# Fourier mixing stage of a two-block network: weights loaded in eight pieces per unit, X and MLP weights loaded earlier, last scatters issued by three engines

## The reference

```python
xn = _layernorm(x, norm1_w, norm1_b)
xf = jnp.fft.rfft2(xn, axes=(1, 2), norm='ortho').reshape(B, h, w // 2 + 1, NB, BS)   # 8 blocks of 24
o1 = jnp.einsum('bhwni,hwnio->bhwno', xf, w1c) + b1c          # w1: (32, 17, 8, 24, 24, 2)
o1 = jax.lax.complex(relu(o1.real), relu(o1.imag)).reshape(B, h, w // 2 + 1, C)
xs = jnp.fft.irfft2(o1, s=(h, w), axes=(1, 2), norm='ortho')
hdn = gelu(_layernorm(xs, norm2_w, norm2_b) @ mlp_w1 + mlp_b1)          # 192 -> 768
return xs + x + hdn @ mlp_w2 + mlp_b2
```

## Time and profile before

| | |
|---|---|
| runs of the kernel | 1224.67 us median of 3 (1222.74 to 1226.86) |
| profiled execution | 1229.31 us, its span 1227.1 us |
| PE busy | 1092.4 us (89%), 9256 matmuls |
| DVE, ACT, POOL busy | 854.0 (70%), 697.0 (57%), 365.5 (30%) |
| mean granted TensorE clock | 0.943 |
| weight queue q1 | 131160 packets, 37.12 MB |
| queue of kind "instruction" q8 | 55 packets, 0.90 MB |
| DMA over the whole span | 64.18 MB, mean 52 GB/s |

### The profile page before, as it was taken

One profiled execution on the slowest core, in us unless ns is written; L12 is line 12 of the kernel. 1 busy time (PEld: TensorE's weight loads), 2 busy tenths in 40 slices (PEclk: granted clock), 3 DMA queues, 4 the chain that ended last, 5 costly groups with the idle time before them and its releaser, 6 DMA issues. The chain is left out here.

```text
span 1227.1 us, 26088 instructions
## 1 busy us (share of the span) xinstructions
PE 1092.4 (89%) x9256; PEld 885.9 (72%) x9256; DVE 854.0 (70%) x2230; ACT 697.0 (57%) x1293; POOL 365.5 (30%) x388
## 2 busy tenths in 40 slices
PE   2549898998578799999979999999999699999998
PEld 1238887887247688899847777767766488989887
DVE  4735544453389988777759769869789767676665
ACT  2545554563365466766676666577554366666665
POOL 1150011111289900000125716527436411111110
PEclk9868888898789899999989999999999889999999
DMA  8977799976300000000010000000000000000001
GB/s 162 317 178 113 142 159 159 151 148 197 82 21 1 1 0 0 0 0 0 0 46 1 1 1 1 1 1 1 1 1 1 0 13 26 26 26 26 26 26 38
DMA packets 138553, 64.18 MB, mean 52 GB/s; under 512 B 114176, under 2 KB 133280, under 8 KB 138464
## 3 DMA queue, kind: packets, MB, share of 16 engines
q1 hardware_dynamic: 131160, 37.12, 16.4%
q0 software_dynamic: 5728, 19.22, 5.9%
q10 hardware_dynamic: 1584, 6.72, 1.7%
HBM read 44.17 MB, written 12.58 MB: 46 GB/s over the span
## 5 line engine op out<-in xcount | busy, mean ns | idle before, releaser
L880 ACT ACTIVATE L_conv_hf<-L_conv_ps,L_conv_b 128x512 f32<-128x512 f32 x192 | 132.0, 688 | 183.4 <-PE L_conv_ps L1051 175.5
L1070 PE MATMUL L_conv_ps<-w2hl,L_conv_hhi 128*128 128x384 f32 x768 | 228.1, 365 | 3.6 <-DVE X L966 3.6
L956 DVE TENSOR_TENSOR L_conv_hlo<-L_conv_hf,L_conv_hhi 128x512 fp32r<-128x512 f32 x192 | 141.3, 751 | 78.1 <-ACT L_conv_hhi L889 75.4
L1070 PE MATMUL L_conv_ps<-w2hl,L_conv_hlo 128*128 128x192 f32 x768 | 188.5, 252 | 0.0
L1185 POOL TENSOR_TENSOR sc_lo<-XS,sc_hi 128x512 fp32r<-128x512 f32 x96 | 142.8, 1503 | 116.4 <-ACT sc_hi L1261 116.4
L1463 PE MATMUL sc_ps<-sc_hi,wh 128*128 128x512 f32 (+1 forms) x440 | 161.0, 437 | 3.4 <-ACT XS L1245 3.2
L621 PE MATMUL psF<-spectrum,X 100*24 100x64 f32 x4352 | 129.5, 290 | 23.7 <-issue 20.2
L1070 PEld LDWEIGHTS L_conv_ps<-w2hl,L_conv_hhi 128*128 128x128 f32 x768 | 144.4, 188 | 7.3 <-DVE L_conv_hlo L956 2.7
L1463 PE MATMUL sc_ps<-sc_hi,wl 128*128 128x512 f32 (+1 forms) x440 | 147.9, 393 | 0.0
L621 PEld LDWEIGHTS psF<-spectrum,X 100*24 100x24 f32 x4352 | 121.6, 122 | 34.9 <-issue 34.7
L1070 PEld LDWEIGHTS L_conv_ps<-w2hl,L_conv_hlo 128*128 128x128 f32 x768 | 146.2, 191 | 0.0
(11 more groups left out here) (135 smaller groups left out, 2052.0 us busy)
## 6 DMA issues: line engine op xcount, KB each, us to landing
X<-in_L_conv_w SPq DMA_DIRECT2D x34, 576.0 KB
XS<-in_x POOLq DMA_DIRECT2D x8, 768.0 KB, 8.2
rows_spectrum<-XS POOLq DMA_DIRECT2D x8, 768.0 KB, 6.7
d<-rows_spectrum ACTq DMA_DIRECT2D x8, 768.0 KB, 7.4
XS<-d POOLq DMA_DIRECT2D x64, 96.0 KB, 6.3
X<-in_x SPq DMA_DIRECT2D x8, 768.0 KB, 6.8
out<-X SPq DMA_DIRECT2D x15, 384.0 KB, 2.6
spectrum<-in_L_conv_mlp_w SPq DMA_DIRECT2D x2, 576.0 KB, 6.0
```

The costliest lines, as they stand in the source:

```text
L880: nc.scalar.activation(hf[:, m % 3, :], ps[:, RB + m % 2, :], gelu, bias=b1[:, m:m + 1]).then_inc(act1, 1)
L956: nc.vector.tensor_tensor(hlo[:, m, :], hf[:, m % 3, :], hhi[:, m, :].bitcast(F32), ALU.subtract).then_inc(h_lo, 1)
L1070: mm = pe.matmul(o, x, w, start=(m == 0 and n == 0), stop=(m == MT - 1 and n == 1), skip_group_check=True)
```

## The change

The weights of a unit go out in eight pieces (four row ranges for each of the two halves), the bias with the first two. `mixed` now counts eight steps per unit, one per 32 products, and piece i of unit u waits for step i of unit u - 2. The pieces of unit 0 wait for the row copies of slabs 4 to 7, those of unit 1 for the second spectrum load. In the last units four slabs of X are issued during the products of unit 15 and the MLP weights during those of unit 16. The other four slabs of X are loaded in inverse_rows, where SP gets a part. The scatters of the last group are issued by SP (three), POOL (three) and ACT (two), each with a semaphore `last_in[k]`; all scatters of the other groups of one parity share one semaphore. Every wait on `mixed` is rescaled. Three lines whose condition is never met are dropped.

```diff
-            sp.wait_ge(x_in[XT - 1], 16)
-            for u in range(UNITS):
+            def load_piece(u, i):
+                r, k, rows = u % RING, i % 2, slice(H // 4 * (i // 2), H // 4 * (i // 2 + 1))
+                s, at = (k, WF - 1) if units[u] is None else (units[u][1], 2 * units[u][0] + k)
+                into = Wt[r][:, k].rearrange("p h o r -> p h (o r)")
+                sp.dma_start(into[0:HALF, rows], w_v[s, at][:, rows]).then_inc(w_in[r], 16)
+                if i < 2:
+                    sp.dma_start(into[HALF:HALF + NH], b_v[s, at]).then_inc(w_in[r], 16)
+
+            for i in range(STEP):
+                sp.wait_ge(d1_done, 2 * TPB + 2 * i)
+                load_piece(0, i)
+            sp.wait_ge(d2_in[1], 16)
+            for i in range(STEP):
+                load_piece(1, i)
+            for u in range(2, UNITS):
+                for i in range(STEP):
+                    sp.wait_ge(mixed, STEP * (u - 2) + i + 1)
+                    load_piece(u, i)
...
-            for u in range(UNITS - RING, UNITS):
-                sp.wait_ge(mixed, 2 * (u + 1))
-                if u == UNITS - 2:
-                    for dst, src in sh.mlp_loads("L0_conv_"):
-                        sp.dma_start(dst, src).then_inc(sh.raw_in, 16)
-                again(u)
+            for n, (u, half) in enumerate(itertools.product((UNITS - 4, UNITS - 3), range(2))):
+                sp.wait_ge(mixed, STEP * (UNITS - 2) + 2 * n + 1)
+                again(u, half)
+            for n, (dst, src) in enumerate(sh.mlp_loads("L0_conv_")):
+                sp.wait_ge(mixed, STEP * (UNITS - 1) + n + 1)
+                sp.dma_start(dst, src).then_inc(sh.raw_in, 16)
+            sp.wait_ge(d3_v, 2 * NG)
+            sp.wait_ge(d3_a, 2 * NG)
+            for k in (0, 3, 6):
+                scatter(sp, NG - 1, k)
...
-                for k in range(TPB):
-                    pool.dma_start(XS[g:P:NG, B * k:B * (k + 1), :].rearrange("p b c -> p (b c)"),
-                                   d3[g % 2][k:P:TPB, :]).then_inc(sh.rows_in[g % 2][k], 16)
+                for k in range(TPB) if g < NG - 1 else (1, 4, 7):
+                    scatter(pool, g, k)
...
+            for k in (2, 5):                      # ACT, after waits for d3_v and d3_a
+                scatter(act, NG - 1, k)
...
-                    if hl % 8 == 7:
+                    if hl % 2 == 1:
                         mm.then_inc(mixed, 1)
...
+        @block.sync                               # in inverse_rows
+        def _(sp):
+            for k in range(TPB):
+                sp.wait_ge(sh.last_in[k], 16)
+            for r in (0, RING - 1):
+                for k in (2 * r, 2 * r + 1):
+                    sp.dma_start(sh.X[:, B * k:B * (k + 1), :], x_v[k]).then_inc(sh.x_back[r], 16)
```

More of the change, by code:

```diff
@@ L149, in __init__ @@
         self.raw_in = self.sem("raw_in")
-        self.rows_in = [[self.sem(f"rows_in{k}_{t_}") for t_ in range(TPB)] for k in range(2)]
+        self.rows_in = [self.sem(f"rows_in{k}") for k in range(2)]
+        self.last_in = [self.sem(f"last_in{t_}") for t_ in range(TPB)]
     def load_table(self, n, func):
@@ L314, in col_bank, with scatter @@
             return 6 if u == 1 else 4
+        def scatter(eng, g, k):
+            eng.dma_start(XS[g:P:NG, B * k:B * (k + 1), :].rearrange("p b c -> p (b c)"),
+                          d3[g % 2][k:P:TPB, :]).then_inc(sh.last_in[k] if g == NG - 1 else sh.rows_in[g % 2], 16)
         block = ctx.enter_context(nc.Block())
@@ L327, in _ @@
                 sp.dma_start(spectrum[k][HALF:HALF + NH, :], t["block_ones"][HALF:HALF + NH, :]).then_inc(ones_in, 16)
-            sp.wait_ge(x_in[XT - 1], 16)
-            for u in range(UNITS):
-                r = u % RING
[L332 to L338, removed]
@@ L437, in rectify @@
                 for q in range(2):
-                    act.wait_ge(mixed, 2 * u + q + 1)
+                    act.wait_ge(mixed, STEP * u + STEP // 2 * (q + 1))
                     nc.scalar.activation(
@@ L446, in inverse_out @@
                 if g >= 2 and half == 0:
-                    for k in range(TPB):
-                        act.wait_ge(sh.rows_in[g % 2][k], 16 * (g // 2))
+                    act.wait_ge(sh.rows_in[g % 2], 16 * TPB * (g // 2))
                 nc.scalar.activation(d3[g % 2][:, 384 * j:384 * j + 384], ps[:, 7, 0:384], ACT.Copy).then_inc(d3_a, 1)
@@ L551, in inverse_out @@
                 if g >= 2 and half == 0:
-                    for k in range(TPB):
-                        dve.wait_ge(sh.rows_in[g % 2][k], 16 * (g // 2))
+                    dve.wait_ge(sh.rows_in[g % 2], 16 * TPB * (g // 2))
                 nc.vector.tensor_copy(d3[g % 2][:, 384 * j:384 * j + 384], ps[:, 6, 0:384]).then_inc(d3_v, 1)
@@ L609, in products @@
                 r = u % RING
-                pe.wait_ge(w_in[r], 64 * (u // RING + 1))
+                pe.wait_ge(w_in[r], 16 * (STEP + 2) * (u // RING + 1))
                 spread_done(u)
@@ L683, in inverse_rows @@
         loads, splits = sh.mlp_loads("L0_conv_"), sh.mlp_splits()
+        x_v = t["x"].rearrange("b (t hh) w c -> t (hh w) b c", hh=HH)
         block = ctx.enter_context(nc.Block())
+        @block.sync
[5 more added lines that the diff above has]
+                    sp.dma_start(sh.X[:, B * k:B * (k + 1), :], x_v[k]).then_inc(sh.x_back[r], 16)
         @block.tensor
         def _(pe):
+            for s in range(2):
+                pe.wait_ge(sh.rows_in[s], 16 * TPB * (NG // 2 - s))
             for k in range(TPB):
-                for s in range(2):
-                    pe.wait_ge(sh.rows_in[s][k], 16 * NG // 2)
+                pe.wait_ge(sh.last_in[k], 16)
                 passed(pe, xs_done, 4 * (k - 1))
```

17 lines of the change are left out of this document (7 added, 10 removed).

## The result

| | before | after |
|---|---|---|
| median of the runs | 1223.70 us | 1198.68 us (1196.19 to 1201.1, 4 runs) |
| ratio | | 0.9774 (95%: 0.9749 to 0.9798) |
| profiled span | 1227.1 us | 1194.4 us |
| start to first product matmul | 89.97 us | 78.75 us |
| first to last product | 213.0 us | 192.9 us |

The change gains 2.3%, or 25 us by the medians (before is four runs here, the three shown ahead and one more). The two profiled executions differ by 32.7 us in their spans: before's profile took 1229.31, longer than any of its four timed runs, and after's is the fastest of its four. So some 8 us of that difference are the choice of executions. In stages the 32.7 are 11.2 + 20.1 + 2.7 - 1.4, up to rounding.

The account below looks back on a forecast made before the run. PE was taken as the bound, slowed by waiting for its own instructions behind weight packets. Savings of 4 + 2.5 + 14.5 - 1 + 4 = 24 us from the median 1224.67 gave 1201 us, range 1190 to 1210 (chance 0.48).

Parts of the forecast that it names:

- the signs promised: Slabs under 6 us apart, first columns near 74, issue near 12, clock above 0.9, last copy to inverse rows near 10.
- Row stage and hand-over: Before the first products: holding weights back saves 4 us on the x slabs and 2.5 us on spectrum landings.
- Units: Products, columns, inverse halves: pieces shrink the weight pile delaying PE's instructions, saving 14.5 us (bounds 34 and -5).
- The two halves of the term: In the units: 7.5 us fewer holes at the products and 7 us less clock loss.
- Odd units: In odd units, which also carry spectrum load and scatter, holes halve from 15.4 us; even units keep 4.8.
- Last units: Units 15 and 16: more X and MLP bytes beside the products cost 1 us; other X loads stay hidden.
- End: Last copy to inverse rows: POOL issues three scatters instead of eight and reaches its DRAIN earlier, gaining 4 us.
- three readings of the DRAIN: At the end: DRAIN lasts 10.08 us from its start, gain 2.4; ends 3.5 after last landing, 6; neither, 9.
- A: In the units: holes vanish altogether, saving 34 us instead of 14.5, for 1181 us; chance 0.17.
- B: In the units: holes stay, as busy DMA engines as such delay the fetch; only 9.5 us gained, 1215; chance 0.22.
- C: In the units: pieces load too slowly and PE waits for weights, 67 us in all, for 1282 us; chance 0.08.
- D: Whole kernel: nothing measurable, gains vanish or holes move to other units, 1222 to 1228 us; chance 0.05.

Follow-up runs that it names:

- e1: The kernel before, with only the weights of units 0 to 3 held back, still as whole transfers; ratio 0.9956, 1221.39 us.
- e2: The changed kernel with units 0 to 3 loaded at the old early start, without pacing; 1200.80 us, ratio 0.9801.
- e3: The changed kernel with all eight pieces of a unit issued at its first step, without pace; 1195.98 us, ratio 0.9768.
- e5: The kernel before with each 576 KB weight transfer cut into four of 144 KB at the old time; 1207.82 us, ratio 0.9858.
- e10: The changed kernel with the four early slabs of X issued as sixteen quarters of 192 KB at the same steps; 1198.38 us, ratio 0.9759.
- e4: The changed kernel with the weights of units 4 to 16 left out; 1190.08 us (one run).
- e7: The changed kernel with all eight slabs of X loaded in the inverse rows; 1192.08 us, ratio 0.9719.
- e8: The changed kernel with the scatters of the last two groups issued by SP and ACT, none by POOL; 1190.68 us, ratio 0.9708.

## Why the prediction was right or wrong

The time was 1198.7 where 1201 stood, and the signs promised came: slabs under 6 us apart (5.97), first columns near 74 (69.7 here, 74.7 on average over the seven kernels with the same late start), "issue" near 12 (11.2), clock above 0.9 (0.93), no wait for a DMA at the products, and a weight queue that runs through them (below, 104 to 108 us). Two were missed: there is still idle time before slabs 5 and 6, and from ACT's last copy to the first inverse-row matmul it is 11.5 us where near 10 stood (14.2 before).

```profile
q1 hardware_dynamic: 3392, 0.64, 91.8%
q8 instruction: 1, 0.02, 1.5%
```

The sum was right partly for wrong reasons, and partly by luck. Its terms were worked out against the profile of before, and in the profiled pair they come to 32.7 instead of 24; the medians of the runs give 25.

**Row stage and hand-over, -6.5.** Right in size, and 11.2 in the profile, where after has the earliest first product of all kernels. Over the profiles of all kernels the first product stands at 89.3 us on average with the early start (89.97, 88.36, 87.56, 87.32, 93.17; 576 KB pieces only in the first) and at 84.0 with the late one (78.75, 82.59, 84.54, 86.36, 86.70, 83.69, 85.50): 5.3, with 6 to 8 between the kernels of each kind. e1, with a late start of whole transfers, has 87.58 and gives 5 alone. The slabs account for less of it than the 4 us that stood: from slab 3 to slab 7 they are on average 6.1 us apart with the late start of the pieces and 6.5 with the early one. What the step left out is the price: units 2 and 3 now load beside units 0 and 1, so that e2, with the early start, is hardly slower than after (2 us by the medians, within the noise).

**Units, -14.5.** It was -20 in the profiled pair (the last units among them), and the mechanism failed in one step. That PE waits for blocks of its instructions beside DMA traffic is right. The step that failed is that such a block waits behind the pile of weights, and that pacing shrinks the pile to one piece. e3 drops the pace and loses nothing; e5 has the old time and the old pile and has the gain. What counts beside the weights is the size of the transfer: the holes go 20.2, 13.2, 8.0 from 576 to 144 KB.

How the size does it stays open. Transfers of 576, 288 and 144 KB take some 3.4, 1.7 and 0.9 us, an estimate from 3072 packets per 576 KB at about 900 per us, and the order of the delays fits a block that waits for the transfer it met. But with pieces of 144 KB the packet's start is still up to 2.3 us late, units 3 and 9 left out, the DMA share falls with the size as well, and e10 speaks against making it a rule for all transfers. The Trainium skill (DMA: Bandwidth & Descriptors, Queues, rings and completion order) lets an engine take turns between queues at packets of some 9 to 17 descriptors; by that the size of a transfer should not matter, and from 576 to 144 KB it mattered by 12 us of holes.

The two halves of the term were both too small. The holes gave 9.0 instead of 7.5, and the clock 11.1 of busy time instead of 7; by the column groups alone, whose excess over 1.99 us fell from 12.4 to 4.6, it is 8.

**Odd units.** Here the step was wrong, and an error the other way hid it in the total. The holes of the odd units were to halve, from 15.4, and those of the even ones to stay at 4.8. In after the odd units have 3.1 left (1.08, 0.28 and 1.78), and the even ones 8.1, of which 4.89 are unit 16's and 1.66 unit 12's. So the drop of "issue" from 20.2 to 11.2, near the 12 forecast, is a sum of -12.3 and +3.3. What remains in units 3 and 9 stands beside the spectrum load: the start of the instruction packet is late there by 1.9 to 4.2 us in all thirteen profiles, and by 2.2 and 1.9 even in e4, where it costs 0.9 us of holes in all. The prediction took unit 1's hole of 1.11 for one beside weights alone; a spectrum load was issued at 103.5 and was moving then too.

**Last units, +1.** Wrong by size: the hole in unit 16 went from 2.15 to 4.89, and e7 puts the price of the X slabs there at 6.6 us by the medians. The other half of that step, the loads hidden in the inverse rows, was right and could have been used for all eight slabs.

**End, -4.** It gave 2.7. Of the three readings of the DRAIN the second is nearest: it ends some 4 to 5 us after the last landing of POOL's own transfers. Before, that is 318.8 and 323.4; after, 284.8 and 289.2; in e8, 269.9 and 273.8. Over all thirteen profiles it is 3.9 to 5.5 us, while the DRAIN is 9.1 to 15.4 long. The step took 314 for the last landing, 4.4 us behind ACT's last copy; it was 284.8, 6.6 behind, as the premise that group 6's scatters are gone by then was false: they stood in POOL's queue ahead of group 7's. The rule of the Trainium skill cited there (DMA: Bandwidth & Descriptors, Issuing engines are not separate DMA queues), that issuing from several engines saves only sequencer time, misses this: taking POOL out of the last two groups is worth 6.7 us, as its DRAIN then ends beside other work.

**The rivals.** A (holes vanish) did not come; e7 comes near it, with 3.4 us of holes and 1192.1. B (the holes stay, whatever the form of the traffic) did not come, and e5 speaks against it; that the share of busy engines plays a part is not excluded, since the share fell with the size. C (pieces too slow) did not come: no product waits for weights, at 72 KB neither, though SP then issues for some 10 us of each unit. D did not come.

## What to carry to other kernels

Where an engine with many small instructions shows gaps that end by "issue", ask what the DMA engines carry at that moment: try smaller transfers first (144 KB instead of 576 KB took 1.4% off this kernel without moving any), then move bulk loads to a stage with idle DMA, as the inverse rows here. Read the packets of kind "instruction" beside the gaps: they tell whether a block came late and what moved before it. Ahead of a barrier, keep the last transfers off POOL: here its DRAIN ended only 4 to 5 us after the last of them had landed. When a pace and a size are changed in one edit, cross them before you credit either: here the pace got the credit in the forecast and the size did the work.

## What the runs showed of the hardware that was not expected

- An instruction block of PE is delayed by other traffic, at its start: PE waited 20.2 us in 213 beside 576 KB transfers of 192-byte runs, and 0.9 us without them (unit 16 left out). It goes on 1.2 to 2.1 us after the end of the 16 KB packet. The Trainium skill (Runtime: NRT & Kernel Launch, Instruction fetch mechanics) calls the crossing of a block mostly hidden; the trace agrees only where the DMA engines have little else to do.
- The gaps seem to cost about as much again by the clock: with 9 us fewer of them the same matmuls took 11 us less busy time in the units, at 0.93 granted instead of 0.87.
- 6.3 MB of X in 768 KB slabs run at some 325 GB/s beside a PE-bound stage without a trace in its time; in the units, where most packets are the weights' 192-byte runs, all traffic together makes 172 GB/s at a DMA share of 0.89.
- POOL's DRAIN lasted 10.08, 9.34 and 15.35 us for the same instruction in before, after and e8, and ended 4.5, 4.4 and 3.9 us after the last of POOL's transfers had landed.
